# Attention: key, value and query-bias products on stacked rounded latents, and a one-pass transpose of the maxima

## The chip, the cores and the metric

One core of one Trainium2 chip runs the whole kernel in one launch. The metric is the device time of that launch in microseconds. Before the change three runs gave 646.17, 646.83 and 647.59 us; the median is 646.83 us. Engines are named as in the profile: PE (TensorE matmul), PEld (its weight loads), DVE (VectorE), ACT (ScalarE), POOL (GpSimd) and SP (which issues the DMAs).

## The reference

Two layers on x of 8 batches x 256 tokens x 128 features; each is an attention-like part and a feed-forward part of experts, under adaLN modulation. The change touches only the attention of layer 0:

```python
h = _layernorm(x, axis=-1) * (1 + ca) + sa
q = (h @ Wq + bq).reshape(B, T, H, D)                 # 16 heads of 8
kv_latent = gelu(h @ Wkd + bkd)                       # 64 wide
lat = kv_latent[..., :L] + kv_latent[..., L:]         # 32 wide
kv = lat @ Wku + bku
k, v = kv[..., :C].reshape(B, T, H, D), kv[..., C:].reshape(B, T, H, D)
attn = softmax(where(causal, q k^T / sqrt(8), -inf))
x = x + ga * ((attn @ v) @ Wo + bo)
```

The feed-forward part of layer 0 routes each token to 2 of 8 experts, beside a shared one (128 to 512 to 128, tanh gelu). Layer 1 is a gated linear recurrence with an MLP, and a second set of experts.

## The kernel before, in words

Everything lives in on-chip memory; features or heads lie on the 128 partitions and tokens along the free axis, in 4 blocks of 512. Each engine runs one instruction list in program order, written out by hand; semaphores join the lists. There is no scheduler, so the order of the source is the order on each engine.

An fp32 product costs TensorE several passes. Where the kernel wants fp32 quality for less, it splits an operand into a rounded part (type fp32r, one pass) and the rest, and adds the products of the parts: a copy into an fp32r tile rounds, and a subtraction of it from the original leaves the rest. `HH`/`HL` are the two parts of the hidden values, `WH`/`WL` those of an expert's weights, `LH`/`LL` those of the layer 1 weights, which lie in `M`.

Start. SP loads V, X (4 blocks), the modulation weights, `KM` (the key and value weights twice, and their bias row: 65 x 640), `M`, and more. PE takes means and variances; DVE centres (L669), copies the modulation out of PSUM (L839 to L851), and normalises block by block (L676, then L680 for each of the two batches in a block, which counts `hn_done`). PE makes the latent of a block (L1285, PSUM bank t), ACT its gelu into `LAT` (L421). Row 64 of `LAT` is one, so that the bias row of `KM` counts. POOL meanwhile sets up masks and identities, flips signs in `KM` (L282, L283; `flipped`) and in the query weights in `M` (L286, L287), rounds the layer 1 weights into `LH` (L289) and, after the second normalised block or later, makes `LL` (L292). PE then projects the first unit, and makes all values (L1400, 16 products of 128 columns, banks 2 to 5), which DVE adds to a bias row (L860). `keep_clock` (L1292) is a row of products whose result nobody reads.

A unit is one batch and 4 of the 16 heads; there are 32. `project` (L1298, L1299, bank 6) makes queries and keys of unit n+3 in plain fp32. ACT evacuates them four times (L432, L434, L436, L437): a kept copy `QKT`, in which only one row group of four survives, and a rounded copy `QKR`; the queries' bias comes in here from `KEPT` and `SIGNED`. POOL subtracts the two (L343, `join`) and so leaves stacked rows of rounded parts and rests, over which PE's `scores` (L1319, L1320) contract in one pass, in two halves h of two heads each in banks 0 and 1. DVE's `maxima` (L874) takes the row maxima of each half, and only then may PE write the next half. `spread_max` (L885, L887) puts the maxima, as rounded part and rest, into `MP`; PE turns them (L1373, `maxima_t`, an fp32 transpose against `IDF`); DVE adds them to the queries (L894, `with_max`). PE makes the transposed scores (L1333, L1334, and the mask L1337), ACT their exponentials (L444), PE the values' sums (L1349, L1352). DVE spreads the sums and divides (L900, L908), ACT takes the reciprocals (L456, L458). After the last units PE runs the output projection (L1364) and the second norm.

Experts of layer 0. POOL splits two experts' weights (L297, L300) and rounds the hidden blocks (L308); DVE takes the hidden rests (L692, `rest`), works out the routing (L768 and on), and takes the rests of the activations (L1015, `lower0`), for which PE waits before each second product.

## Time and profile before

| quantity | value |
|---|---|
| median of 3 runs | 646.83 us (646.17 to 647.59) |
| the profiled execution, whole | 646.88 us |
| its span, first to last instruction | 645.0 us |
| mean granted TensorE clock | 0.967 of full speed |
| busy PE, DVE, ACT, POOL | 599.1, 542.1, 487.6, 167.7 us |

The profiled execution took 646.88 us, of which 645.0 us is the span; the other 1.9 us lie around it. Busy times are sums over stages with different limits. The attention's units run from about 37 to 184 us, the first experts from about 204 us on. A row of the timeline says when an instruction starts, how long it takes, its engine, line and operation, and in brackets how long the engine had stood idle and on whom it waited.

### The profile page before, as it was taken

How to read it: one execution, taken by the hardware profiler on the slowest of the kernel's cores; microseconds unless marked ns; L12 is line 12 of the kernel's file. 1: busy time of each engine (PE TensorE's matmuls, PEld its weight loads, DVE VectorE, ACT ScalarE, POOL GpSimd, SP SyncE). 2: the span in 40 equal slices, each digit the busy share in tenths (PEclk: the TensorE clock that was granted, in tenths of full speed). 3: DMA queues.
4: the chain of work that ended last, by engine and by line, in shares of the span. 5: the costliest groups of instructions: out<-in, count | busy, mean ns of one | idle time of the engine just before them, and what ended most of it. 6: DMA issues, size and time to landing. Idle time of an engine off the chain costs nothing.

```text
span 645.0 us, 10999 instructions
## 1 busy us (share of the span) xinstructions
PE 599.1 (93%) x3297; PEld 441.4 (68%) x3297; DVE 542.1 (84%) x1338; ACT 487.6 (76%) x858; POOL 167.7 (26%) x144
## 2 busy tenths in 40 slices
PE   8799889888999999999999999785898999999996
PEld 5466556555545688888888888354675888888884
DVE  4868888888858868988988888869799789999997
ACT  5658999999647899999999999798635556666663
POOL 4422323223304033553455342040432000000000
PEclk9899999999998999999999999996897999999998
DMA  7000000000100042112201210000000222222201
GB/s 252 1 1 3 1 3 1 1 0 1 34 1 0 6 164 99 52 47 99 98 29 68 98 49 1 1 1 1 0 1 2 69 91 89 91 90 90 91 0 67
DMA packets 6491, 28.83 MB, mean 45 GB/s; under 512 B 862, under 2 KB 990, under 8 KB 4383
## 3 DMA queue, kind: packets, MB, share of 16 engines
q1 hardware_dynamic: 6448, 28.32, 12.4%
q8 instruction: 19, 0.31, 0.2%
q14 instruction: 24, 0.20, 0.1%
HBM read 27.13 MB, written 1.19 MB: 44 GB/s over the span
## 4 chain that ended last, share of the span: by engine, by line
PE 63%; DVE 24%; ACT 6%; issue 4%; DMA 1%; POOL 0%; SPq 0%; DVEq 0%; ACTq 0%; POOLq 0%
PE PS L1213 17%; PE PS L1215 16%; PE PS L1214 16%; DVE STAT L874 9%; PE PS L1364 2%; PE PS L1292 2%; DVE RA L894 2%; PE PS L1319 2%; PE PS L1239 2%; DVE SU L900 1%; DVE HN L680 1%; PE PS L1333 1%; ACT STAT L397 1%; DVE HL L692 1%; ACT RA L635 1%
## 5 line engine op out<-in xcount | busy, mean ns | idle before, releaser
L1015 DVE TENSOR_TENSOR RA<-AR,RA 128x512 fp32r<-128x512 f32 x144 | 137.4, 978 | 26.2 <-ACT RA L518 24.6
L517 ACT ACTIVATE AR<-PS,BI 128x512 f32<-128x512 f32 x144 | 99.8, 693 | 15.3 <-PE PS L1215 7.8
L1213 PE MATMUL PS<-HH,WH 128*128 128x512 f32 x272 | 108.9, 400 | 0.2
L1215 PE MATMUL PS<-HL,WH 128*128 128x512 f32 x272 | 107.1, 394 | 0.0
L1214 PE MATMUL PS<-HH,WL 128*128 128x512 f32 x272 | 107.1, 394 | 0.0
L518 ACT ACTIVATE RA<-PS,BI 128x512 fp32r<-128x512 f32 x144 | 98.7, 685 | 0.0
L874 DVE CUSTOM_DVE_ANT_0 STAT<-PS,MQ 128x128 f32<-128x128 f32 (+1 forms) x256 | 76.3, 355 | 20.0 <-PE PS L1320 19.9
L1213 PE MATMUL PS<-RA,WH 128*128 128x512 f32 x208 | 83.0, 399 | 3.7 <-DVE RA L1179 2.1
L1215 PE MATMUL PS<-RA,WH 128*128 128x512 f32 x208 | 81.2, 391 | 0.0
L1214 PE MATMUL PS<-RA,WL 128*128 128x512 f32 x208 | 81.2, 391 | 0.0
L320 POOL TENSOR_TENSOR AR<-AR 128x512 f32<-128x512 f32 x32 | 50.8, 1587 | 113.2 <-DVE AR L827 113.2
L343 POOL TENSOR_TENSOR RA<-QKT,RA 128x512 fp32r<-128x512 f32 x32 | 40.7, 1273 | 102.8 <-ACT RA L437 99.7
L635 ACT ACTIVATE RA<-AR 128x512 fp32r<-128x512 f32 x64 | 40.5, 633 | 32.8 <-DVE AR L1173 32.1
L1213 PEld LDWEIGHTS PS<-HH,WH 128*128 128x128 f32 x272 | 51.9, 191 | 12.8 <-issue 1.7
L1214 PEld LDWEIGHTS PS<-HH,WL 128*128 128x128 f32 x272 | 51.9, 191 | 11.1 <-issue 0.5
L1215 PEld LDWEIGHTS PS<-HL,WH 128*128 128x128 f32 x272 | 51.8, 190 | 11.1
L444 ACT ACTIVATE AR<-PS 128x768 f32<-128x768 f32 x64 | 48.5, 810 | 13.3 <-PE PS L1337 11.3
L629 ACT ACTIVATE AR<-PS 128x512 f32<-128x512 f32 x64 | 38.3, 598 | 20.7 <-PE PS L1215 19.2
L1213 PEld LDWEIGHTS PS<-RA,WH 128*128 128x128 f32 x208 | 39.1, 188 | 15.8 <-DVE RA L1015 5.1
L1179 DVE TENSOR_TENSOR RA<-AR,RA 128x512 fp32r<-128x512 f32 x64 | 44.2, 690 | 5.7 <-ACT RA L635 1.3
L1161 DVE TENSOR_TENSOR AR<-PS,AR 128x512 f32<-128x512 f32 x64 | 43.9, 687 | 4.2 <-ACT AR L629 3.6
L1215 PEld LDWEIGHTS PS<-RA,WH 128*128 128x128 f32 x208 | 39.2, 188 | 8.3
(212 smaller groups left out, 1164.3 us busy)
## 6 DMA issues: line engine op xcount, KB each, us to landing
...
```

Of the source, the lines that this page charges most:

```text
L320: gp.tensor_tensor(out=blk(ACC, t), in0=blk(ACC, t), in1=YW[:, t % 2, :], op=ALU.add)\
L444: act.activation(PR[:, n0 % 2, 2 * h:2 * h + 2, :], PS[:, 2 + 2 * h:4 + 2 * h, 0:384], ACT.Exp, scale=SCALE).then_inc(exp_done, 1)
L517: act.activation(G[:, c, :], PS[:, c, :], ACT.Gelu_apprx_tanh, bias=bias).then_inc(s["act"], 1)
L518: act.activation(GH[:, m0 % 2, c, :], PS[:, c, :], ACT.Gelu_apprx_tanh, bias=bias)\
L635: act.activation(GH[:, m % 2, c, :], G[:, c, :], ACT.Copy).then_inc(s1["gh"], 1)
L874: mm = dve.tensor_tensor_reduce(out=MASKED_S[:, q, j, 0:width], in0=PS[:, j, first:first + width], in1=MQ[:, 256 - width:256], scale=-1.0, ...
L1015: dve.tensor_tensor(out=GL[:, m0 % 2, c, :], in0=G[:, c, :], in1=f(GH[:, m0 % 2, c, :]), op=ALU.subtract).then_inc(s["lo"], 1)
L1161: dve.tensor_tensor(out=G[:, c, :], in0=PS[:, 2 + c, :], in1=SG[:, c, :], op=ALU.mult)\
L1179: dve.tensor_tensor(out=GL[:, m % 2, c, :], in0=G[:, c, :], in1=f(GH[:, m % 2, c, :]), op=ALU.subtract).then_inc(s1["lo"], 1)
L1213: pe.matmul(out, wh, xh, start=first, stop=False)
L1214: pe.matmul(out, wl, xh, start=False, stop=False)
L1215: return pe.matmul(out, wh, xl, start=False, stop=last)
```

## The change

The rounded parts and rests of the latents are made once, instead of multiplying keys and values in plain fp32 for each unit.

- `kmats` grows from 65 x 640 to 98 x 1250: three stacked copies of the key and value weights and two bias rows, the queries' bias in rows 96 and 97 of columns 640 to 1151, and a 0/1 matrix `pick` in the last 98 columns. `KM` now lies in the big tile AR.
- POOL flips signs in the queries' bias too, and splits that bias (three operations of 512 columns and two small ones). DVE splits the key and value weights into `KMS` (two operations of 640 columns), ahead of the copy of the modulation.
- The gelu's output goes to `LG`. A new product, `three_rows`, multiplies it by `pick` in plain fp32 and so adds the two halves of the latent and stacks them three times (98 rows, over the latent's bank). DVE's new `latents` reads that twice and leaves rounded parts and rests in `LAT`.
- `project` is the query's fp32 product, plus a one-pass product of the bias rows into the same bank, plus a one-pass key product. The values' 16 products are one-pass.
- ACT evacuates a unit in three operations instead of four: no bias, and both rounded copies in one operation of 512 columns.
- `maxima_t` multiplies `MP` by a rounded identity `IDR` in one pass.
- `LL` is no longer made at the start but on POOL after the last hidden block of the first experts has been rounded.

The diff, without the packing of the inputs on the host and the declarations:

```diff
@@ gpsimd
+            gp.wait_ge(ident_done, 9)
+            gp.tensor_scalar(IDR, IDF[:, :], 1.0, 0.0, ALU.mult, ALU.add).then_inc(ident_done, 1)
...
+            qb = KM[:, 640:1152].rearrange("p (h r c) -> p h r c", r=4, c=8)
+            gp.tensor_scalar(qb[:, :, 0, :], qb[:, :, 0, :], -1.0, 0.0, ALU.mult, ALU.add).then_inc(qk_bias, 1)
+            gp.tensor_scalar(qb[:, :, 2:4, :], qb[:, :, 2:4, :], -1.0, 0.0, ALU.mult, ALU.add).then_inc(qk_bias, 1)
+            gp.wait_ge(in_vec, 16)
+            gp.wait_ge(qk_bias, 2)
+            gp.tensor_scalar(KMR[:, 640:1152], KM[:, 640:1152], vec("w_sign")[0:98, :], 0.0, ALU.mult, ALU.add).then_inc(qk_bias, 1)
+            gp.tensor_scalar(KM[:, 640:1152], KM[:, 640:1152], vec("w_keep")[0:98, :], 0.0, ALU.mult, ALU.add).then_inc(qk_bias, 1)
+            gp.wait_ge(qk_bias, 4)
+            gp.tensor_tensor(out=KMS[:, 640:1152], in0=KM[:, 640:1152], in1=f(KMR[:, 640:1152]), op=ALU.subtract)\
+              .then_inc(qk_bias, 1)
...
-            gp.wait_ge(l1_split, 1)
-            gp.wait_ge(hn_done, 8)
-            gp.tensor_tensor(out=LL[:, :], in0=lm, in1=f(LH[:, :]), op=ALU.subtract).then_inc(l1_split, 1)
...
             split_weights(0, 1, 1, 1024)
             split_hidden(1, HN, 3)
+            gp.wait_ge(l1_split, 1)
+            gp.tensor_tensor(out=LL[:, :], in0=lm, in1=f(LH[:, :]), op=ALU.subtract).then_inc(l1_split, 1)
             experts(0, E0, 1024)
@@ scalar, evac_proj
-                act.activation(QKT[:, 0, :], PS[:, 6, 0:256], ACT.Identity,
-                               bias=KEPT[:, g:g + 1], scale=vec("q_keep")).then_inc(qk_evac, 1)
-                act.activation(QKR[:, 0, :], PS[:, 6, 0:256], ACT.Identity,
-                               bias=SIGNED[:, g:g + 1]).then_inc(qk_evac, 1)
+                act.activation(QKT[:, 0, :], PS[:, 6, 0:256], ACT.Copy, scale=vec("q_keep")).then_inc(qk_evac, 1)
                 act.activation(QKT[:, 1, :], PS[:, 6, 256:512], ACT.Copy, scale=vec("k_keep")).then_inc(qk_evac, 1)
-                act.activation(QKR[:, 1, :], PS[:, 6, 256:512], ACT.Copy).then_inc(qk_evac, 1)
+                act.activation(QKR[:, :, :], PS[:, 6, :].rearrange("p (k n) -> p k n", k=2), ACT.Copy).then_inc(qk_evac, 2)
@@ vector
             for t in range(NBLK):
                 centre(0, t)
+            dve.wait_ge(flipped, 2)
+            dve.tensor_scalar(KMR[:, 0:640], KM[:, 0:640], vec("w_sign")[0:98, :], None, ALU.mult).then_inc(kms_done, 1)
+            dve.wait_ge(kms_done, 1)
+            dve.scalar_tensor_tensor(out=KMS[:, 0:640], in0=KM[:, 0:640], scalar=vec("w_keep")[0:98, :], in1=f(KMR[:, 0:640]),
+                                     op0=ALU.mult, op1=ALU.subtract).then_inc(kms_done, 1)
...
+            def latents(t):
+                dve.wait_ge(sel_psum, t + 1)
+                if t >= 1:
+                    dve.wait_ge(l_done, t)
+                dve.tensor_scalar(LATR, PS[0:98, t, :], vec("lat_sign")[0:98, :], None, ALU.mult).then_inc(lr_done, 1)
+                dve.wait_ge(lr_done, t + 1)
+                dve.scalar_tensor_tensor(out=blk(LAT, t), in0=PS[0:98, t, :], scalar=vec("lat_keep")[0:98, :],
+                                         in1=f(LATR), op0=ALU.mult, op1=ALU.subtract).then_inc(l_done, 1)
+            for t in range(NBLK):
+                latents(t)
@@ tensor
+            def three_rows(t):
...
+                pe.wait_ge(lat_done, t + 1)
+                pe.matmul(PS[0:98, t, :], KM[0:65, 1152:1250], blk(LG, t), start=True, stop=True).then_inc(sel_psum, 1)
+            for t in range(3):
+                latent(t)
+            three_rows(0)
+            latent(3)
+            three_rows(1)
+            three_rows(2)
@@ project
-                pe.matmul(PS[:, 6, 0:256], mat("wq", g), HN[:, cols], start=True, stop=True)
-                pe.matmul(PS[:, 6, 256:512], KM[:, 128 * g:128 * g + 128], LAT[:, cols], start=True, stop=True)\
+                pe.matmul(PS[:, 6, 0:256], mat("wq", g), HN[:, cols], start=True, stop=False)
+                pe.matmul(PS[:, 6, 0:256], KMS[:, 640 + 128 * g:768 + 128 * g], LAT[:, cols], start=False, stop=True)
+                pe.matmul(PS[:, 6, 256:512], KMS[:, 128 * g:128 * g + 128], LAT[:, cols], start=True, stop=True)\
@@ maxima_t
-                    mm = pe.transpose(PS[:, 7, 256 + 128 * q:384 + 128 * q], f(MP[:, q, :]), IDF[:, :])
+                    mm = pe.matmul(PS[:, 7, 256 + 128 * q:384 + 128 * q], MP[:, q, :], IDR, start=True, stop=True)
@@ before the first unit
-            pe.wait_ge(lat_done, 1)
+            pe.wait_ge(kms_done, 2)
+            pe.wait_ge(qk_bias, 5)
+            pe.wait_ge(l_done, 1)
             project(0, 0, 0)
-            pe.wait_ge(lat_done, 4)
+            three_rows(3)
             for i in range(16):
+                if i % 4 == 0:
+                    pe.wait_ge(l_done, min(i // 4 + 3, 4))
```

POOL before, from the arrival of `KM` to the first join; AR and RA are the big tiles in which the new `KM`, `KMS` and `KMR` lie.

```order
L282 TENSOR_SCALAR KM<-KM 65x16x16 [waits in_k]
L283 TENSOR_SCALAR KM<-KM 65x16x8
L286 TENSOR_SCALAR M<-M 128x16x8 [waits in_mats]
L287 TENSOR_SCALAR M<-M 128x16x16
L289 TENSOR_SCALAR LH<-M 128x1664
L292 TENSOR_TENSOR LL<-M,LH 128x1664 [waits hn_done,l1_split]
L343 TENSOR_TENSOR RA<-QKT,RA 128x512 [waits qk_evac] x4
```

POOL after, the same place.

```order
L290 TENSOR_SCALAR AR<-AR 98x16x16 [waits in_k]
L291 TENSOR_SCALAR AR<-AR 98x16x8
L293 TENSOR_SCALAR AR<-AR 98x16x8
L294 TENSOR_SCALAR AR<-AR 98x16x16
L297 TENSOR_SCALAR RA<-AR,V 98x512 [waits qk_bias,in_vec]
L298 TENSOR_SCALAR AR<-AR,V 98x512
L300 TENSOR_TENSOR RA<-AR,RA 98x512 [waits qk_bias]
L304 TENSOR_SCALAR M<-M 128x16x8 [waits in_mats]
L305 TENSOR_SCALAR M<-M 128x16x16
L307 TENSOR_SCALAR LH<-M 128x1664
L358 TENSOR_TENSOR RA<-QKT,RA 128x512 [waits qk_evac] x4
```

Five operations on `KM` and the queries' bias now stand ahead of the query weights and `LH`, and `LL` is gone from here.

DVE before, from the last centring to the first normalised block.

```order
L669 TENSOR_TENSOR XC<-X,PS 128x512 [waits mean_done] x3
L839 COPY MOD<-PS 128x96 [waits mod_psum]
L840 TENSOR_SCALAR MC<-PS 128x32
L843 TENSOR_SCALAR GS<-MOD 128x32 [waits mod_done]
L845 SCALAR_TENSOR_TENSOR GA<-MOD 128x16 x2
L849 TENSOR_SCALAR GA<-GA 128x32 [waits gate_done]
L851 SCALAR_TENSOR_TENSOR MG<-GS,GA 128x32 [waits gate_done]
L676 TENSOR_TENSOR HN<-XC,STAT 128x512 [waits rstd_done]
L680 TENSOR_SCALAR HN<-HN,MC,MOD 128x256 [waits nrm_done]
```

DVE after, the same place.

```order
L681 TENSOR_TENSOR XC<-X,PS 128x512 [waits mean_done] x3
L848 TENSOR_SCALAR RA<-AR,V 98x640 [waits flipped]
L850 SCALAR_TENSOR_TENSOR RA<-AR,V,RA 98x640 [waits kms_done]
L855 COPY MOD<-PS 128x96 [waits mod_psum]
L856 TENSOR_SCALAR MC<-PS 128x32
L859 TENSOR_SCALAR GS<-MOD 128x32 [waits mod_done]
L861 SCALAR_TENSOR_TENSOR GA<-MOD 128x16 x2
L865 TENSOR_SCALAR GA<-GA 128x32 [waits gate_done]
L867 SCALAR_TENSOR_TENSOR MG<-GS,GA 128x32 [waits gate_done]
L688 TENSOR_TENSOR HN<-XC,STAT 128x512 [waits rstd_done]
L692 TENSOR_SCALAR HN<-HN,MC,MOD 128x256 [waits nrm_done]
```

The two operations of 640 columns stand between the centring and the copy of the modulation, and wait for POOL's `flipped`.

POOL before, from the last unit's neighbours to the first experts.

```order
L300 TENSOR_TENSOR WL<-WS,WH 128x1024 [waits moe0_split]
L308 TENSOR_SCALAR HH<-HN 128x512 [waits hn_done] x3
L297 TENSOR_SCALAR WH<-WS 128x1024 [waits moe0_w_in]
L300 TENSOR_TENSOR WL<-WS,WH 128x1024 [waits moe0_split]
L308 TENSOR_SCALAR HH<-HN 128x512 [waits hn_done]
L320 TENSOR_TENSOR AR<-AR 128x512 [waits moe0_ymul,moe0_acc_init]
```

POOL after, the same place.

```order
L315 TENSOR_TENSOR WL<-WS,WH 128x1024 [waits moe0_split]
L323 TENSOR_SCALAR HH<-HN 128x512 [waits hn_done] x3
L312 TENSOR_SCALAR WH<-WS 128x1024 [waits moe0_w_in]
L315 TENSOR_TENSOR WL<-WS,WH 128x1024 [waits moe0_split]
L323 TENSOR_SCALAR HH<-HN 128x512 [waits hn_done]
L374 TENSOR_TENSOR LL<-M,LH 128x1664 [waits l1_split]
L335 TENSOR_TENSOR AR<-AR 128x512 [waits moe0_ymul,moe0_acc_init]
```

`LL`, a subtraction of 1664 columns with both inputs in SBUF, stands right behind the rounding of the last hidden block, which DVE's `rest` of that block waits for.

## Rows read from the trace of the kernel before

**Rows 1.** Waits, 57 to 166 us: who waited for whom, us, times, longest.

```profile
DVE STAT L874 <- PE PS L1320: 15.0, 25, 0.6
PE PS L1319 <- DVE NM L874: 4.7, 25, 0.2
```

**Rows 2.** Timeline, one unit; start, us, engine, line; idle in brackets.

```profile
102.20 0.29 DVE L874 CUSTOM_DVE_ANT_0 STAT<-PS,MQ 128x128 f32<-128x128 f32 x1 [0.60 <-PE PS L1320]
...
103.43 0.18 DVE L885 CAST MP<-NM 128x8 fp32r<-128x8 f32 x1
...
103.49 0.60 PE L1299 MATMUL PS<-AR,KM 65*128 x2
...
103.93 0.39 PE L1373 MATMUL PS<-IDF,MP 128*128 128x128 f32 x2
...
104.44 0.41 DVE L894 TENSOR_TENSOR RA<-RA,PS 128x256 fp32r<-128x256 f32 x1
...
107.82 0.17 DVE L885 CAST MP<-NM 128x8 fp32r<-128x8 f32 x1
```

**Rows 3.** Timeline, end of the units, POOL and DVE.

```profile
170.45 2.35 POOL L300 TENSOR_TENSOR WL<-WS,WH 128x1024 fp32r<-128x1024 f32 x1
170.50 2.32 DVE L887 TENSOR_TENSOR MP<-NM,MP 128x8 f32<-128x8 f32 x1
```

**Rows 4.** Timeline, the start, POOL and DVE.

```profile
11.85 0.40 POOL L282 TENSOR_SCALAR KM<-KM 65x256 f32<-65x256 f32 x1 [6.08 <-DMA KM<-in_kmats]
...
13.82 0.26 DVE L839 COPY MOD<-PS 128x96 f32<-128x96 f32 x1 [3.78 <-PE PS L1276]
...
14.97 0.79 POOL L286 TENSOR_SCALAR M<-M 128x128 f32<-128x128 f32 x1 [2.46 <-DMA M<-in_mats]
15.64 2.21 DVE L680 TENSOR_SCALAR HN<-HN,MC,MOD 128x256 f32<-128x256 f32 x2
...
16.10 1.61 POOL L289 TENSOR_SCALAR LH<-M 128x1664 fp32r<-128x1664 f32 x1
...
21.23 0.73 DVE L680 TENSOR_SCALAR HN<-HN,MC,MOD 128x256 f32<-128x256 f32 x2
...
22.12 3.70 POOL L292 TENSOR_TENSOR LL<-M,LH 128x1664 fp32r<-128x1664 f32 x1 [4.41 <-DVE HN L680]
22.14 3.70 DVE L949 SCALAR_TENSOR_TENSOR SP<-V,SP 128x1 f32<-128x1 f32 x1
```

**Rows 5.** Chain that ended last, 28 to 36 us: start, us, what.

```profile
28.58 0.33 PE PS L1319 x2
...
30.17 0.57 ACT QKT L432
...
31.80 1.18 PE PS L1298 x2
...
33.83 2.56 PE PS L1292 x8
```

**Rows 6.** Busy time by stretch: us; PE, PEld, DVE, ACT, POOL; PEclk, DMA, GB/s.

```profile
11.00:15.00 4.00, 4.00 (x28) 3.30 (x28) 1.07 (x8) 3.03 (x6) 0.69 (x3) 0.98 0.83 332
28.00:32.00 4.00, 2.32 (x14) 1.51 (x14) 2.89 (x16) 1.57 (x4) 0.55 (x2) 0.98 0.00 0
32.00:35.00 3.00, 3.00 (x8) 2.36 (x9) 1.32 (x4) 1.13 (x3) 1.15 (x1) 0.50 0.00 0
```

**Rows 7.** Timeline, the first experts' start.

```profile
208.34 0.62 POOL L308 TENSOR_SCALAR HH<-HN 128x512 fp32r<-128x512 f32 x1 [2.01 <-DVE HN L680]
...
208.99 0.69 DVE L692 TENSOR_TENSOR HL<-HN,HH 128x512 fp32r<-128x512 f32 x1 [0.74 <-POOL HH L308]
...
210.13 0.68 DVE L1015 TENSOR_TENSOR RA<-AR,RA 128x512 fp32r<-128x512 f32 x1
...
210.87 0.50 PE L1213 MATMUL PS<-RA,WH 128*128 128x512 f32 x1 [0.69 <-DVE RA L1015]
```

**Rows 8.** Busy time by stretch, as rows 6.

```profile
212.00:216.00 4.00, 3.78 (x17) 2.52 (x16) 3.81 (x13) 4.00 (x9) 0.00 (x0) 1.00 0.00 0
```

More of the change, by code:

```diff
@@ L12 @@
 MASKED = -1e30
[L15 to L16 removed]
+VECS = dict(bo=1, q_keep=1, k_keep=1, b1=4 * E0, b2=E0, pb=4, gb=3, fb=3,
+            outb=1, alpha=1, norm=1, norm2=1, bkd=1, c=16, prio=8,
+            w_sign=1, w_keep=1, lat_sign=1, lat_keep=1)
 MATS = dict(wkd=64, wq=512, wo=512, router=8, wg=8, l1=4 * 128 + 3 * 384)
@@ L92, in build @@
         ON = AR[:, 0:8192].rearrange("p (g n) -> p g n", g=4)
-        LAT = AR[0:65, 8192:10240]
+        LG = AR[0:65, 8192:10240]
+        KM = AR[0:98, 2048:3298]
         VALL = AR[:, 10240:12288].rearrange("p (i c) -> p i c", i=16)
@@ L102, in build @@
         QKR = RA[:, 2560:3072].rearrange("p (k n) -> p k n", k=2)
+        IDR = RA[:, 7936:8064]
+        LAT = RA[0:98, 3072:5120]
+        KMS = RA[0:98, 5120:6272]
+        KMR = RA[0:98, 6272:7424]
+        LATR = RA[0:98, 7424:7936]
         MASKED_S = STAT[:, 0:1024].rearrange("p (q j n) -> p q j n", q=2, j=2)
         QKT = sb("QKT", [128, 2, 256])
-        KEPT = sb("KEPT", [128, 4])
-        SIGNED = sb("SIGNED", [128, 4])
         NM = sb("NM", [128, 8])
@@ L420, in _ @@
                 act.wait_ge(kd_done, t + 1)
-                act.activation(LAT[0:64, t * BLK:(t + 1) * BLK], PS[0:64, t, :], ACT.Gelu, bias=vec("bkd")[0:64, :])\
+                act.activation(LG[0:64, t * BLK:(t + 1) * BLK], PS[0:64, t, :], ACT.Gelu, bias=vec("bkd")[0:64, :])\
                    .then_inc(lat_done, 1)
             def evac_proj(n, g):
-                if isinstance(n, int) and n == 0:
-                    act.wait_ge(qk_bias, 2)
                 act.wait_ge(proj_done, n + 1)
@@ L886, in spread_max @@
                 dve.wait_ge(mp_ready, 2 * n + 1)
-                dve.tensor_tensor(out=f(MP[:, :, 25::32]), in0=nmv, in1=f(MP[:, :, 24::32]),
+                dve.tensor_tensor(out=MP[:, :, 25::32], in0=nmv, in1=f(MP[:, :, 24::32]),
                                   op=ALU.subtract).then_inc(mp_ready, 1)
@@ L1282, in _, with latent @@
             pe.wait_ge(in_mats, 16)
-            for t in range(NBLK):
+            def latent(t):
                 pe.wait_ge(hn_done, 2 * t + 2)
@@ L1286, in _ @@
                   .then_inc(kd_done, 1)
+            def three_rows(t):
+                if t == 0:
+                    pe.wait_ge(in_k, 16)
+                    pe.wait_ge(latent_one, 1)
+                pe.wait_ge(lat_done, t + 1)
[6 more added lines that the diff above has]
+            three_rows(2)
             def keep_clock(count, bank=7):
@@ L1681, in layouts @@
     put("bkd", a["L0_attn_bkd"])
+    put("w_sign", np.repeat(np.array([-1, -1, 1, -1, 1], f4), [32, 32, 32, 1, 1]))
+    put("w_keep", np.repeat(np.array([0, 0, 1, 0, 1], f4), [32, 32, 32, 1, 1]))
+    put("lat_sign", np.repeat(np.array([-1, 1, -1, -1], f4), [32, 32, 32, 2]))
+    put("lat_keep", np.repeat(np.array([0, 1, 0, 0], f4), [32, 32, 32, 2]))
     put("c", np.concatenate([a["L0_c"], a["L1_c"]]).T)
@@ L1694, in layouts @@
     wk = np.concatenate([heads(a["L0_attn_Wku"][:, :128], 3).reshape(32, 512), a["L0_attn_Wku"][:, 128:]], 1)
+    bias = np.concatenate([bk.reshape(1, 512), np.zeros((1, 128), f4)], 1)
+    pick = np.zeros((98, 98), f4)
+    pick[np.arange(192) % 64, np.arange(192) // 64 * 32 + np.arange(192) % 32] = 1.0
+    pick[64, 96:98] = 1.0
+    qb = np.concatenate([np.zeros((96, 512), f4), np.tile(heads(a["L0_attn_bq"], 3).reshape(1, 512), (2, 1))])
     rows = np.concatenate([a["L0_attn_bku"][128:], a["L0_ffn_router_b"]])
```

19 lines of the change are left out of this document (5 added, 14 removed).

## The prediction, made before the changed kernel was run

> **What bounds the kernel now.** I read four views, in this order. The waits over the middle of the attention say who stands still: DVE's `maxima` waits for the second half of the scores once a unit, 25 times in 109 us, 0.60 us each [rows 1, 2]; no other wait of DVE is among the long ones. The timeline of one unit says why: from one L885 to the next it takes 4.39 us (103.43 to 107.82), and DVE is busy in all of it but those 0.60 us. The wait is a round trip: PE may write the second half only when the first half's maxima are taken, and PE itself stands idle before that product (4.7 us in 25 times, 0.2 each) [rows 1]. So DVE plus this round trip is the period, not PE, though PE is the busiest engine of the page. Third, the start of the program, where the order of POOL and DVE decides. Fourth, the start of the first experts, where DVE is busy 3.81 of 4 us, ACT 4.00 and PE 3.78 [rows 8]: nobody has room there.
>
> **The loop.** Per unit PE loses a key product in plain fp32 (0.43 us from L1299 to L1373 [rows 2]) and gains two one-pass products of 256 columns. Eight such products of 512 columns took at least 2.56 us, half of it at half clock [rows 5, 6], so one of 256 costs at most 0.16; PE saves 0.11 to 0.43, I take 0.2. ACT saves an instruction of four, 0 to 0.41 (a quarter of the 1.63 us from 30.17 to 31.80 [rows 5]), I take 0.15. The one-pass transposes end at most some 0.3 us earlier. DVE's instructions are the same ones. The turned maxima are wanted at 104.44, when DVE comes to L894 without a wait; PE started on them at 103.93 [rows 2]. Being earlier there is worth nothing, and being later by more than a few tenths would cost; a 128-column product on the same operands doesn't look slower. The 0.60 us round trip consists of scores alone, which don't change. So the loop is worth 0 (between -0.1 and +0.1 us a unit, 3 us either way over 28 units), and the saved PE and ACT time becomes idle time.
>
> **Two engines, one path to SBUF.** The costs below rest on a behaviour that the trace shows three times. At the end of the units DVE's subtraction of 8 columns, 0.17 us elsewhere, took 2.32 us, exactly as long as POOL's `WL` beside it [rows 3]. L949 on one column took 3.70 us beside POOL's `LL` of 3.70 [rows 4]. And two L680, 0.73 us later on, took 2.21 beside POOL's `LH` [rows 4]. The small instruction waited for all of the large one. The Trainium skill says so too (SBUF — State Buffer, "SBUF: two separate sides"): an exclusive lock, held for the whole instruction by whoever starts first, against a DVE instruction with two SBUF inputs or in a two-port mode. The trace agrees; were it a sharing of bandwidth, `LL` would stretch its neighbours by tenths, not by microseconds.
>
> **The start, step by step.** (1) `KM` grows from 162.5 to 478.5 KB and `M` lies behind it in SP's queue. At 332 GB/s [rows 6] that is 1.0 us: `KM` at 12.8 instead of 11.85, `M` at 15.9 instead of 14.97 [rows 4]. (2) POOL now has, between the two, four small sign flips (0.40 for 256 columns [rows 4]; 1.2 in all), two operations of 512 columns (1.61 x 512/1664 = 0.5 each) and a subtraction (3.70 x 512/1664 = 1.1): 3.3 us; then as before the query flips and `LH`, 2.2 us. (3) DVE gets two operations of 640 columns (0.69 x 640/512 = 0.86 each [rows 7]), which wait for `flipped`, some 13.4 at the earliest. Queued behind them are the copy of the modulation (13.82 before [rows 4]), five small operations on it, and the first normalised block, for which PE and everything later wait. Lower end: 13.4 + 1.7 = 15.1, 1.3 us later than 13.82. Upper end: every such DVE instruction takes turns with a POOL one, 12.8 + 5.5 + 1.7 + 1.4 (normalising) + 0.6 (small ones) = 22.0 against 17.85 before, 4.2 later. Walking both queues with turns I come to 21.1, so +3.2: the small operations each let one of POOL's by, and `LH` falls, as before, into the first block. (4) The last block is then normalised at 25.2 instead of 21.96. From there the first scores took 6.6 us (28.58 [rows 5]). Now a stacking product must come first (1.4 us until PE has got to it, behind a latent at half clock), then DVE's eight operations of 512 columns, 0.69 each and a semaphore between, 5.7 us, of which the value products wait for the last, and 12 of these, 1.2 us at 0.1: 8.3 us, at most, 7.4 where the stacking product is ready. I take 8.1: +1.5. No cover for it: ACT's evacuation and POOL's join of unit 0 are done by then. What goes is `LL` beside L949, which nobody waited for. (5) Up to the first unit, two projections and one evacuation are on the path: -0.2, -0.2, -0.2. The filler products behind them ran at half clock in part, after a stretch in which PE was busy 2.32 of 4 us [rows 6]; if the clock stays up, 1.3 us more go, if it falls longer, as much is lost. I take -0.6. The start: 3.2 + 1.5 - 0.6 = **+4.1**, from +1 to +6.
>
> **The end of the units.** POOL reaches the experts' first weights some 0.3 us earlier, so the 2.32 us of blocking [rows 3] begin and end earlier: **-0.3** (0 to -0.5).
>
> **`LL` at its new place.** It takes 3.70 us with its port [rows 4] and starts when L308 ends, at 208.96; DVE's L692 for the same block is released by the same event and started at 208.99 [rows 7]. If POOL is first, L692 ends 3.6 us later. If DVE is first, L692, a product read out of PSUM and a reduction pass, and L1015 at 210.13, with both inputs in SBUF, waits till 213.1: 3.0. Behind L1015 stand the routing and all further L1015; PE waited for this very one, 0.69 us until 210.87 [rows 7]. DVE, ACT and PE are full from there on [rows 8], so nothing catches up: I take **+3.3**. PE then stands idle nearly 4 us. When it had been busy 2.32 us of 4 the granted clock went to 0.50, the 1.2 GHz level, for about 3 us [rows 6]; the same here costs up to half of 3.4 us of PE's work, and PE sets the pace: **+1.0** (0 to +2.5). The Trainium skill (TensorE: Matmul & The Clock Gate, "HAM oscillation — how this bites in real kernels") speaks of the same: an engine that has to wait restarts cold, and the wait is paid again. The trace agrees, with these rows.
>
> **The sum** against the profiled execution: 646.88 (645.0 of span and 1.9 around it, at the median of the runs, 646.83) + 4.1 + 0 - 0.3 + 3.3 + 1.0 = 655.0 us.
>
> **Rivals.**
>
> *A, the block at the experts is hidden.* `LL` meets no DVE instruction that needs the path, or the engines have more room than rows 8 say. Only the start remains: 646.9 + 4.1 - 0.3 + 0.3 = 651.0. For it: PE idled 0.69 us there. Against it: three blocked instructions in rows 3 and 4.
>
> *B, the start is cheap.* The small operations pass POOL, data arrive no later, and the new DVE work fills the 3.78 us in which DVE stood idle before 13.82 [rows 4]: +1 in place of 4.1, 651.9. Against it: that idle time is mostly over when `KM` arrives.
>
> *C, the loop is bound by PE after all.* Every unit DVE is released by PE [rows 1]; if what ends the 0.60 us is PE's queue and not the round trip, the wait shrinks by what PE saves, up to 0.4 us with both edits. Over 28 units that is -11.2: 646.9 + 8.1 - 11.2 = 643.8, faster than before. It decides from 0.3 us a unit. Against it are PE's own 0.2 us of idleness just before [rows 1].
>
> *D, the clock falls again.* With less PE work per unit, a long wait for the last latent and the idle stretch at the experts, two or three more stretches at half clock: +4, 659. For it: it fell after 2.32 of 4 us. Against it: in the units PE is still busy most of the time.
>
> **How the numbers follow.** The forecast 0.56, A 0.13, B 0.14, C 0.07, D 0.10. The forecast's own range is 653 to 657.5. Eight in ten, with A and B taken in and part of D: 649.8 to 659. A difference of 0.2% (1.3 us) is about what these measurements tell from none. Faster: C, 0.07. The same: the gentle end of B with A, 0.04. Slower: 0.89.
>
> **What would show it.** In the changed profile: the copy of the modulation at 15 us or later, POOL and DVE in turns with instructions stretched up to the neighbour's end, and the first normalised block 1.3 to 4.2 us late; the first scores at 33 us (28.58 before); a unit still of 4.39 us with the 0.60 us wait in it, and new idle time of PE before the transposes and of ACT before its evacuation; `LL` at the experts' start beside an L692 or L1015 (under their new line numbers) of over 3.5 us, a PE that waits for it some 4 us, and a clock at 0.50 behind it. A unit shorter than 4.2 us would prove me wrong in the loop, and first scores before 31 us in the start.

## The result, and the profile after

The changed kernel takes 658.29 us, median of 4 runs (657.57 to 659.06), against 646.69 us for the kernel before in the same session (646.17 to 647.59): ratio 1.0178, 95% interval 1.0160 to 1.0196. It is slower, by 11.6 us. The forecast was 655.0, 8.1 us slower; its own range was 653 to 657.5, the wider one, with parts of the rivals in it, 649.8 to 659. Some single executions of the changed kernel's variants have a long stretch at a lower clock; the ratios leave them out, and of `a4_rows`, whose profiled execution was such a one from 123 us on, only the start is read.

The profiled execution took 658.58 us, span 656.7, mean clock 0.960. When the same event comes in both traces (line before / line after):

| event | before | after | difference |
|---|---|---|---|
| POOL's first flip, `KM` has landed (L282 / L290) | 11.85 | 13.51 | +1.7 |
| first block normalised (end of the second L680 / L692) | 17.85 | 21.84 | +4.0 |
| last block normalised | 21.96 | 25.95 | +4.0 |
| first maxima (L874 / L904) | 29.11 | 37.09 | +8.0 |
| last unit's maxima leave (L885 / L915) | 178.21 | 185.89 | +7.7 |
| first activation rest (L1015 / L1042) | 210.13 | 221.29 | +11.2 |
| the 61st of these | 292.35 | 305.04 | +12.7 |
| end of the span | 645.0 | 656.7 | +11.7 |

So 8.0 us arise ahead of the first maxima, 0.3 come back over the units, 3.5 arise at the experts' start, 1.5 just behind it, and 1.0 comes back later.

These are differences of two single traces, and the start scatters. In the eight profiled kernels whose start is the old one or nearly so (the kernel before and, of the experiments below, `b1_ll_late`, `b2_load`, `b3_turn`, `c1_early`, `c2_placed`, `e1_nokey` and `e2_dve`) the first maxima come at 28.9 to 31.3 us, and the trace of the kernel before, with 29.11, is one of the early ones; after the change they come at 37.1. From the first maxima to the end of the span it takes 619.4 to 619.7 us in the three kernels that make `LL` at the experts (the changed one, `a3_both_late`, `b1_ll_late`) and 614.7 to 616.8 in the eight that make it at the start and whose loop and experts are not slowed or rearranged otherwise (`before`, `a1_ll_back`, `a5_all`, `b2_load`, `b3_turn`, `b5_split`, `c1_early`, `e1_nokey`). The two places of loss stand clear of this scatter; single microseconds in the table don't.

The start, timeline, POOL and DVE; it answers to [rows 4]: start, length, engine, line, and in brackets the idle time and its releaser.

```profile
13.51 0.41 POOL L290 TENSOR_SCALAR AR<-AR 98x256 f32<-98x256 f32 x1 [7.34 <-DMA AR<-in_kmats]
...
14.21 0.57 DVE L848 TENSOR_SCALAR RA<-AR,V 98x640 fp32r<-98x640 f32 x1 [2.34 <-POOL AR L291]
14.82 0.89 DVE L850 SCALAR_TENSOR_TENSOR RA<-AR,V,RA 98x640 fp32r<-98x640 f32 x1
15.63 0.24 DVE L855 COPY MOD<-PS 128x96 f32<-128x96 f32 x1
...
17.03 1.31 POOL L300 TENSOR_TENSOR RA<-AR,RA 98x512 fp32r<-98x512 f32 x1
17.13 3.94 DVE L688 TENSOR_TENSOR HN<-XC,STAT 128x512 f32<-128x512 f32 x1
...
18.95 1.58 POOL L307 TENSOR_SCALAR LH<-M 128x1664 fp32r<-128x1664 f32 x1
```

DVE's first normalising operation, 0.69 us elsewhere, takes 3.94. It starts 0.10 us after POOL's L300 and ends 0.54 us after POOL's L307 has ended (20.53). Between them POOL ran four instructions in a row (L300, L304, L305, L307), and DVE got in between none of them. The prediction had reckoned with turns.

From the last block to the first maxima, timeline, PE and DVE.

```profile
27.00 1.10 PE L1322 MATMUL PS<-AR 65*98 65x512 f32 x2
...
28.14 0.75 DVE L879 TENSOR_SCALAR RA<-PS,V 98x512 fp32r<-98x512 f32 x1 [2.19 <-PE PS L1322]
...
34.25 0.75 DVE L881 SCALAR_TENSOR_TENSOR RA<-PS,V,RA 98x512 fp32r<-98x512 f32 x1
...
35.06 1.55 PE L1446 MATMUL PS<-RA 98*128 98x128 f32 x12 [0.99 <-DVE RA L881]
...
36.54 0.33 PE L1363 MATMUL PS<-RA 32*128 32x128 f32 x2
...
37.09 0.29 DVE L904 CUSTOM_DVE_ANT_0 STAT<-PS,MQ 128x128 f32<-128x128 f32 x1 [0.59 <-PE PS L1364]
```

DVE waits 2.19 us for the first stacking product, then does the eight operations of `latents` from 28.14 to 35.00, and the last twelve value products and the scores stand behind them. The clock shows in the busy times by stretch (us; PE, PEld, DVE, ACT, POOL; clock, DMA share, GB/s), the second row of which answers to the ladder at half clock in [rows 6]:

```profile
22.00:26.00 4.00, 4.00 (x5) 1.07 (x6) 3.84 (x9) 1.01 (x2) 0.00 (x0) 0.50 0.00 0
...
36.00:44.00 8.00, 7.31 (x29) 5.71 (x29) 4.47 (x20) 2.65 (x6) 2.08 (x2) 0.57 0.01 3
217.00:222.00 5.00, 0.82 (x4) 0.35 (x3) 4.97 (x6) 2.08 (x4) 3.29 (x1) 0.58 0.00 0
222.00:226.00 4.00, 3.97 (x9) 3.17 (x10) 3.76 (x13) 2.28 (x4) 0.00 (x0) 0.50 0.00 0
```

The loop, waits from 65 to 174 us, who waited for whom (total, times, longest); it answers to [rows 1]:

```profile
DVE STAT L904 <- PE PS L1364: 15.0, 25, 0.6
ACT AR L456 <- PE PS L1381: 14.2, 25, 0.6
...
PE PS L1363 <- DVE NM L904: 4.6, 25, 0.2
```

and one unit of it, timeline, as [rows 2]:

```profile
102.33 0.17 DVE L915 CAST MP<-NM 128x8 fp32r<-128x8 f32 x1
...
102.85 0.43 PE L1417 MATMUL PS<-RA,MP 128*128 128x128 f32 x2
...
103.60 0.41 DVE L924 TENSOR_TENSOR RA<-RA,PS 128x256 fp32r<-128x256 f32 x1
...
106.95 0.18 DVE L915 CAST MP<-NM 128x8 fp32r<-128x8 f32 x1
...
111.33 0.17 DVE L915 CAST MP<-NM 128x8 fp32r<-128x8 f32 x1
```

DVE waits for the scores the same 15.0 us in 25 units, a unit takes 4.38 us (106.95 to 111.33; the one before it, 4.62, has the placing of new values in it), and what ACT has saved has become a wait of its own, 14.2 us. The turned maxima are ready at 103.28, and L924 comes at 103.60, when DVE gets to it.

The end of the units, timeline, as [rows 3]:

```profile
177.80 2.35 POOL L315 TENSOR_TENSOR WL<-WS,WH 128x1024 fp32r<-128x1024 f32 x1
178.03 2.15 DVE L915 CAST MP<-NM 128x8 fp32r<-128x8 f32 x1
```

The small operation waits for the split as before, another line and 0.17 us less.

The first experts, timeline, as [rows 7]:

```profile
216.59 3.71 POOL L374 TENSOR_TENSOR LL<-M,LH 128x1664 fp32r<-128x1664 f32 x1
216.66 4.18 DVE L704 TENSOR_TENSOR HL<-HN,HH 128x512 fp32r<-128x512 f32 x1 [0.74 <-POOL HH L323]
...
221.29 0.68 DVE L1042 TENSOR_TENSOR RA<-AR,RA 128x512 fp32r<-128x512 f32 x1
...
222.03 0.80 PE L1240 MATMUL PS<-RA,WH 128*128 128x512 f32 x1 [4.20 <-DVE RA L1042]
```

POOL was first; the rest of the last hidden block (0.69 us before) took 4.18, and PE stood 4.20 us for the operation behind it (0.69 before).

### The profile page after: what moved, and what is told of

The parts are those of the page before. It is cut to its first block, busy times and chain, and to the rows that moved or that the text cites. A ratio compares the mean times of both kernels' runs of the same rounds, so it can differ in the third digit from the quotient of the medians.

```text
span 656.7 us, 10968 instructions
## 1 busy us (share of the span) xinstructions
PE 601.9 (92%) x3289; PEld 445.7 (68%) x3289; DVE 551.2 (84%) x1346; ACT 478.7 (73%) x826; POOL 171.0 (26%) x150
## 4 chain that ended last, share of the span: by engine, by line
PE 63%; DVE 24%; ACT 6%; issue 5%; DMA 2%; SPq 0%; POOL 0%; DVEq 0%; ACTq 0%
PE PS L1240 17%; PE PS L1241 16%; PE PS L1242 16%; DVE STAT L904 9%; PE PS L1408 2%; PE PS L1335 2%; DVE RA L924 2%; PE PS L1363 2%; DMA AR<-in_kmats 2%; DVE HN L688 1%; DVE SU L930 1%; DVE HL L704 1%; ACT STAT L414 1%; PE PS L1377 1%; PE PS L1266 1%
## 5 line engine op out<-in xcount | busy, mean ns | idle before, releaser
L1042 DVE TENSOR_TENSOR RA<-AR,RA 128x512 fp32r<-128x512 f32 x144 | 137.7, 980 | 25.9 <-ACT RA L530 24.5
L904 DVE CUSTOM_DVE_ANT_0 STAT<-PS,MQ 128x128 f32<-128x128 f32 (+1 forms) x256 | 76.2, 354 | 19.1 <-PE PS L1364 19.1
L456 ACT ACTIVATE AR<-PS 128x768 f32<-128x768 f32 x64 | 48.4, 809 | 24.1 <-PE PS L1381 24.1
L1240 PEld LDWEIGHTS PS<-HH,WH 128*128 128x128 f32 x272 | 51.9, 191 | 12.7 <-issue 1.9
L1241 PEld LDWEIGHTS PS<-HH,WL 128*128 128x128 f32 x272 | 52.0, 191 | 10.6 <-issue 0.2
```

The lines of the kernel that those rows point to most:

```text
L456: act.activation(PR[:, n0 % 2, 2 * h:2 * h + 2, :], PS[:, 2 + 2 * h:4 + 2 * h, 0:384], ACT.Exp, scale=SCALE).then_inc(exp_done, 1)
L904: mm = dve.tensor_tensor_reduce(out=MASKED_S[:, q, j, 0:width], in0=PS[:, j, first:first + width], in1=MQ[:, 256 - width:256], scale=-1.0, ...
L1042: dve.tensor_tensor(out=GL[:, m0 % 2, c, :], in0=G[:, c, :], in1=f(GH[:, m0 % 2, c, :]), op=ALU.subtract).then_inc(s["lo"], 1)
L1240: pe.matmul(out, wh, xh, start=first, stop=False)
L1241: pe.matmul(out, wl, xh, start=False, stop=False)
```

## The experiments

Each ratio is against the kernel before, timed beside it on the same chip. `a` is an edit of the changed kernel, `b`, `c` and `e` of the kernel before.

### b1_ll_late, the move of `LL` alone

```diff
-            gp.wait_ge(l1_split, 1)
-            gp.wait_ge(hn_done, 8)
-            gp.tensor_tensor(out=LL[:, :], in0=lm, in1=f(LH[:, :]), op=ALU.subtract).then_inc(l1_split, 1)
...
             split_hidden(1, HN, 3)
+            gp.wait_ge(l1_split, 1)
+            gp.tensor_tensor(out=LL[:, :], in0=lm, in1=f(LH[:, :]), op=ALU.subtract).then_inc(l1_split, 1)
```

> The kernel before with nothing changed but the place of LL, behind the last hidden block of the first experts. Theory (exclusive path): +3.5 us for the blocked subtraction, and 0 to +1.6 for the clock: 650.2 to 652, with an L692 of over 4 us beside it. Rival 1 (it only hurts in the changed kernel, whose phases differ): 646.5 to 647.5. Rival 2 (bandwidth is shared, the neighbours stretch by tenths): 647 to 647.7.

Measured: 651.12 us, ratio 1.0053 (1.0030 to 1.0077), 3.4 us slower. Its timeline:

```profile
211.09 3.71 POOL L356 TENSOR_TENSOR LL<-M,LH 128x1664 fp32r<-128x1664 f32 x1
211.16 4.19 DVE L691 TENSOR_TENSOR HL<-HN,HH 128x512 fp32r<-128x512 f32 x1 [0.74 <-POOL HH L305]
...
215.80 0.68 DVE L1014 TENSOR_TENSOR RA<-AR,RA 128x512 fp32r<-128x512 f32 x1
```

The operation behind starts 4.64 us after the rest does, against 1.14 before [rows 7], and the price is passed on nearly whole. For the clock behind it little is left: from the first to the 61st activation rest it takes 82.8 us, against 82.2 before (up to 82.6 in other kernels with `LL` at the start) and 83.8 after the change.

### a1_ll_back, everything but the move of `LL`

The same edit backwards, on the changed kernel.

> The changed kernel with LL made on POOL at the start again, behind LH and the second normalised block. Theory (the exclusive path between POOL and DVE, and the clock behind it): the 4.18 us L704 falls to about 0.7, the 4.20 us in which PE waited at the first experts go, and so does the half clock behind it: 3.5 us for the wait and 1.6 for the clock, 653.2 us (652.5 to 654.5). At the start LL now lies beside DVE's latents, which read PSUM and one tile of SBUF: nothing is blocked there. Rival 1 (the engines catch up elsewhere, LL is a symptom): 657.5 to 658.5. Rival 2 (LL blocks the latents just as it blocked the rest): what is won at the experts is lost at the start, 657 to 658, and an L879 or L881 of 3 to 4 us.

Measured: ratio 1.0127 (1.0082 to 1.0172), so some 3.3 us of the 11.6 are gone, with a wide interval; the theory had 5. The timeline at the experts:

```profile
218.47 0.69 DVE L705 TENSOR_TENSOR HL<-HN,HH 128x512 fp32r<-128x512 f32 x1 [0.74 <-POOL HH L326]
...
219.61 0.68 DVE L1043 TENSOR_TENSOR RA<-AR,RA 128x512 fp32r<-128x512 f32 x1
```

The block is away, and from the first maxima (38.12) to here it takes 181.5 us, as before (181.0); after the change it is 184.2. `LL` waits for the fourth normalised block (`hn_done` counts two for each), so at the start it now ran from 27.31 to 31.01, beside the first operations of `latents`, and these kept their 0.75 us. They have one operand in PSUM. The Trainium skill (SBUF — State Buffer, "SBUF: two separate sides") says that a DVE operation with two inputs in SBUF, or in a two-port mode, and a POOL operation shut each other out. The trace agrees for the inputs: 0.75 here, 4.18 where both were in SBUF.

### a3_both_late, the splitting moved behind the normalising

```diff
-            dve.wait_ge(flipped, 2)
-            dve.tensor_scalar(KMR[:, 0:640], ...)
-            dve.scalar_tensor_tensor(out=KMS[:, 0:640], ...)
             dve.wait_ge(mod_psum, 1)
...
             for t in range(NBLK):
                 normalise(0, t)
+            (the same lines)
```

and POOL's five operations on the queries' bias behind `LH`.

> The changed kernel with two moves at the start: DVE's two operations on the key weights stand behind the fourth normalised block, where DVE waited 2.19 us for the first stacking product, and POOL's split of the queries' bias (two flips, two operations of 512 columns, one subtraction) stands behind LH. Theory (the run of POOL instructions held the path and DVE's L688 waited 3.94 us for all of it): L688 is then at most some 2 us long, the first normalised block is ready 2.5 to 3.5 us earlier, and the whole is 655 us (654.3 to 656). Rival 1 (the start is bound by the arrival of the inputs): at most 0.5 us is won, 657.8 to 658.3. Rival 2 (the latents' chain on DVE and the half clock bind): the earlier first block is given back behind it, 656.8 to 658.

Measured: 658.21 us, ratio 1.0164 (1.0136 to 1.0192): no gain that can be told from none, though the first block was normalised 4.1 us earlier (17.72). The timeline says where it went:

```profile
18.36 2.22 DVE L692 TENSOR_SCALAR HN<-HN,MC,MOD 128x256 f32<-128x256 f32 x2
...
23.08 2.02 DVE L692 TENSOR_SCALAR HN<-HN,MC,MOD 128x256 f32<-128x256 f32 x2
...
25.59 0.88 DVE L871 SCALAR_TENSOR_TENSOR RA<-AR,V,RA 98x640 fp32r<-98x640 f32 x1
26.39 0.74 DVE L879 TENSOR_SCALAR RA<-PS,V 98x512 fp32r<-98x512 f32 x1
...
32.91 2.82 PE L1446 MATMUL PS<-RA 98*128 98x128 f32 x12 [0.98 <-DVE RA L881]
...
36.51 0.29 DVE L904 CUSTOM_DVE_ANT_0 STAT<-PS,MQ 128x128 f32<-128x128 f32 x1 [1.75 <-PE PS L1364]
```

Most of it is lost before the last block: two pairs of normalising operations, 0.73 us elsewhere, now wait beside `LH` (18.82 to 20.43) and beside POOL's moved splitting (to 24.94), and the last block is ready at 25.09, only 0.9 us earlier. The two DVE operations then stand between it and `latents`, which end at 32.85, and the value products behind ran at half clock, 2.82 us instead of 1.55. The first maxima are 0.6 us earlier. This is the second rival's outcome, by a longer road.

### b5_split, the splitting alone, on the kernel before

```diff
+            gp.wait_ge(flipped, 2)
+            gp.tensor_scalar(<128 columns>) ; gp.tensor_scalar(<256 columns>)
+            gp.tensor_scalar(<512 columns>) ; gp.tensor_scalar(<512 columns>)
+            gp.tensor_tensor(<512 columns>, op=ALU.subtract)
...
+            dve.wait_ge(flipped, 2)
+            dve.tensor_scalar(RA[0:65, 6272:6912], KM[:, 0:640], 1.0, None, ALU.mult).then_inc(kms_done, 1)
+            dve.wait_ge(kms_done, 1)
+            dve.scalar_tensor_tensor(out=RA[0:65, 5120:5760], in0=KM[:, 0:640], scalar=1.0,
+                                     in1=f(RA[0:65, 6272:6912]), op0=ALU.mult, op1=ALU.subtract).then_inc(kms_done, 1)
             dve.wait_ge(mod_psum, 1)
```

> The kernel before, with the new splitting work alone: behind POOL's sign flips two small copies, two copies of 512 columns and a subtraction of 512, and on DVE, ahead of the copy of the modulation, a rounding and a subtraction of 640 columns that wait for the flips. Their results go to unused columns and are read by nobody. Nothing is loaded in addition, so KM lands as before. Theory 1 (the queue at the start is the mis-sized part, and it is passed on whole): the first normalise of the first block takes over 3 us beside POOL's row of instructions, the first normalised block is 3 to 4.5 us late, the last one as well, and the time is 3 to 4.5 us longer, 650 to 651.5 us. Theory 2 (the start is dear only through the chain over the latents): the first block is late by 1 to 4 us but the time is at most 1.5 us longer.

Measured: 649.17 us (12 runs), ratio 1.0019 (1.0004 to 1.0033): 1.2 us. Theory 1 has fallen, theory 2 holds. Its timeline:

```profile
11.49 0.40 POOL L283 TENSOR_SCALAR KM<-KM 65x256 f32<-65x256 f32 x1 [5.71 <-DMA KM<-in_kmats]
...
12.91 0.89 DVE L851 SCALAR_TENSOR_TENSOR RA<-KM,RA 65x640 fp32r<-65x640 f32 x1
16.06 0.26 DVE L855 COPY MOD<-PS 128x96 f32<-128x96 f32 x1 [2.25 <-PE PS L1292]
...
16.45 2.00 DVE L859 TENSOR_SCALAR GS<-MOD 128x32 f32<-128x32 f32 x1
```

`KM` lands at 11.49, as in the kernel before, and both DVE operations are over before the modulation is there; DVE even waits 2.25 us for it. What is left is one small operation that waited for POOL, 2.00 us for 32 columns. The first block is normalised at 20.41, 2.6 us later than in the trace of the kernel before, but 1.2 later than in the middle one of the eight with the old start (17.6 to 20.0, median 19.2), which is what the times say. After the change, with `KM` at 13.51, it is 21.84.

### b2_load and a4_rows, the load

`b2_load` is the kernel before with `KM` padded to 128 x 896, 448 KB. `a4_rows` is the changed kernel with `kmats` padded from 98 to 128 rows of the same 5000 bytes, 625 KB.

> The kernel before with a larger load for KM (128 x 896 elements, 448 KB instead of 162.5; the added columns and rows are zeros and are not used). Theory (the load takes its share of the channel from those issued ahead of it and behind it): the last block of X, KM and M arrive about 1 us later; M alone gates nothing for long, the modulation product is up to 1.5 us later and with it the first normalised block: +0.5 to +1.5 us, 647.3 to 648.3. Rival (loads behind each other in the queue are served in order and DVE waits for something else anyway): 646.5 to 647.0. If it is over 649, the load is the main cost of the start.

> The changed kernel with the KM load padded from 98 to 128 rows of 5000 bytes (625 KB instead of 478.5), on the 128 partitions that the other loads have; the added rows are zeros. The 448 KB load of 128 rows cost the kernel before nothing and landed at 11.3 us, while the 98-row load landed at 13.4 to 14.4. Theory (the 98-row shape, not its bytes, makes the start late, because the first blocks of X and the modulation weights also arrive 1 to 2 us late with it): KM lands at 12 to 12.5, the last centring ends before 10.5 instead of 11.9, the whole 656.5 to 657.5. Rival (bytes): 0.5 us later than the changed kernel, 658.5 to 659.5. Rival (the start's lateness is on DVE and POOL alone): 658 to 658.5.

Measured: `b2_load` 647.3 us, ratio 0.9998 (0.9971 to 1.0026), the weights there at 11.32. `a4_rows` 1.0155 (1.0118 to 1.0191); the weights were there at 11.64, and the first maxima at 35.67, 1.4 us earlier than after the change. The last centring did not end earlier as forecast, but at 12.45. The busy time by stretch from 9 to 12.75 us, columns as above, shows the loads; after the change:

```profile
9.00:12.75 3.75, 3.75 (x11) 1.63 (x9) 2.06 (x3) 1.32 (x2) 0.00 (x0) 1.00 1.02 248
```

and in `a4_rows`:

```profile
9.00:12.75 3.75, 3.75 (x8) 1.62 (x7) 2.36 (x4) 0.81 (x3) 1.10 (x4) 1.00 1.03 434
```

While the load of 98 rows was under way, all loads together moved 248 GB/s, with 128 rows 434, though these carry more bytes. Four profiled executions with 98 rows had the weights at 13.51, 14.44, 14.72 and 15.38; none with 65 or 128 rows had them later than 12.62. So at 5000 bytes a row it is the 98 rows that make them late, not the size. The Trainium skill (DMA: Bandwidth & Descriptors, "Why a DMA increments its semaphore by 16 and not by 1") says that a transfer is dealt to the largest number of engines up to 16 that divides its outer dimension: 14 for 98 rows, 16 for 128. The trace doesn't bear that out as the whole cause: the DMA share of 1.02, against 1.03, shows no idle engines; 14 of 16 of 434 would still be 380; and 65 rows, 13 engines by the same rule, weren't late. Why 98 rows are slow stays open. How much of the 11.6 us it is stays open too: the total differs from the changed kernel's by less than the intervals tell.

### a5_all, the three moves undone together

> The changed kernel with all three moves undone together: LL at the start behind LH, DVE's splitting of the key and value weights behind the normalising, POOL's splitting of the bias behind LH. What is left of the change is the stacking, the latents, the one-pass products, the evacuation in three instructions and the larger load. If the excess of 11.6 us is the sum of its parts (LL and the clock behind it 5, the queue ahead of the first block 1 to 4): 650 to 653 us, still 3 to 6 us slower than before, because the latents' chain stays and the loop gives nothing. Rival (the loop's savings are only covered up by the three moves): 647 us or less. Second rival (the moves trade places with one another and the queue merely reappears): 656 us or more.

Measured: 657.7 us, ratio 1.0169 (1.0130 to 1.0208), the second rival. Timeline, POOL and DVE:

```profile
26.18 3.87 POOL L310 TENSOR_TENSOR LL<-M,LH 128x1664 fp32r<-128x1664 f32 x1 [0.29 <-DVE HN L693]
26.54 4.20 DVE L872 SCALAR_TENSOR_TENSOR RA<-AR,V,RA 98x640 fp32r<-98x640 f32 x1
...
40.88 0.29 DVE L905 CUSTOM_DVE_ANT_0 STAT<-PS,MQ 128x128 f32<-128x128 f32 x1 [1.75 <-PE PS L1365]
```

and its busy time by stretch, columns as above:

```profile
32.00:49.00 17.00, 15.34 (x48) 11.51 (x48) 10.22 (x30) 3.98 (x9) 3.82 (x3) 0.50 0.01 1
```

`LL` left the experts and met the moved subtraction of the key weights, both of whose inputs are in SBUF: 4.20 us, right ahead of `latents`. PE stood idle for 3.28 us meanwhile, until 32.33, and its clock was at half from 31.9 us for 17 us. From the first maxima on this variant is as fast as the kernel before (181.5 us to the first activation rest, 184.2 after the change); up to them it is 11.8 us later.

### e1_nokey, b3_turn and e2_dve, who sets the loop

`e1_nokey` leaves out the key product from the fifth unit on; `b3_turn` takes the one-pass transposes alone; `e2_dve` adds a copy to DVE in 28 units:

```diff
+                if n0 >= 4:
+                    dve.tensor_copy(STAT[:, 1024:1152], MQ[:, 0:128])
```

> The kernel before; from the fifth unit on the key product is left out (queries and keys of the later units are then not those of the reference), so PE has 0.43 us less to do in each of 28 units, more than the change saves it, and the same is queued on all other engines. Theory (a unit is DVE's work plus a round trip of 0.60 us): the period stays 4.39 us, the whole 646.2 to 647.5. Rival (PE's queue sets the unit): up to 0.4 us less in each of 28 units, 635 to 640.

> The kernel before, with the one-pass transposes of the maxima alone (one rounded identity more on POOL early in the start, and DVE leaves the maxima's rest in a rounded type). Forecast: DVE is the engine that sets the unit, and comes to the turned maxima without a wait, so the period stays 4.38 to 4.40 us and the time within 0.2% of before, 646 to 648 us. Rival (what DVE waits for in its 0.6 us is PE's queue): the transposes are 0.1 to 0.3 us shorter a unit, the time falls by 3 to 8 us.

> The kernel before with one more DVE copy of 128 columns in each of the last 28 units, behind L894; its result is not used. Theory (DVE sets the unit): its 0.15 to 0.22 us is paid in every unit, 4.39 becomes 4.55 to 4.6 us, the whole 651 to 653. Rival (the unit has room on DVE, PE or ACT sets it): 646.5 to 647.5.

Measured: `e1_nokey` 0.9996 (0.9980 to 1.0013), `b3_turn` 0.9997 (0.9980 to 1.0014), `e2_dve` 1.0042 (1.0025 to 1.0058), 2.7 us slower. One row of the timeline each a unit apart; `e1_nokey`:

```profile
103.22 0.17 DVE L885 CAST MP<-NM 128x8 fp32r<-128x8 f32 x1
107.60 0.17 DVE L885 CAST MP<-NM 128x8 fp32r<-128x8 f32 x1
```

`b3_turn`:

```profile
100.26 0.17 DVE L889 CAST MP<-NM 128x8 fp32r<-128x8 f32 x1
104.65 0.18 DVE L889 CAST MP<-NM 128x8 fp32r<-128x8 f32 x1
```

`e2_dve`:

```profile
101.74 0.17 DVE L885 CAST MP<-NM 128x8 fp32r<-128x8 f32 x1
106.23 0.17 DVE L885 CAST MP<-NM 128x8 fp32r<-128x8 f32 x1
```

Less work for PE leaves the period at 4.38 and 4.39 us; one small operation more on DVE makes it 4.49. That is less than the forecast of 4.55 to 4.6: the copy takes 0.22 us, but the next operation starts 0.13 after it, and the 0.60 us wait stays. DVE with its round trip sets the loop, and rival C has fallen.

### c1_early and c2_placed, the second expert's split on the kernel before

```diff
             split_weights(0, 0, 0, 1024)
-            for t in range(3):
+            gp.wait_ge(moe[0]["w_in"], 32)
+            split_weights(0, 1, 1, 1024)
+            for t in range(4):
                 split_hidden(1, HN, t)
-            gp.wait_ge(moe[0]["w_in"], 32)
-            split_weights(0, 1, 1, 1024)
-            split_hidden(1, HN, 3)
```

`c1_early` is this. `c2_placed` also makes the first expert's split behind the first join instead of behind the last, and the second's only when all maxima have left.

> The kernel before with POOL's two weight splits of the first experts moved: the first expert's from behind the last join to behind the first, where DVE works from PSUM; the second's from between the hidden blocks to behind the last unit's L887. Theory (exclusive path): L887 takes 0.17 instead of 2.32 us, the three L692 2.1 instead of 4.94 us, together 4 to 5 us, part of it in places where PE was the later one: 642.5 to 644. Rival 1 (PE's output projections bind there): 645.5 to 647. Rival 2 (the split behind join 0 delays the first units by as much): 645 to 646.5.

> The kernel before; POOL splits the second expert's weights right behind the first's, ahead of the first three hidden blocks, instead of behind them. The variant that did this and also moved the first expert's split into the attention took 645.6 us, 0.997 of before. If its gain is the freed way for the last hidden block at the experts' start: this one gains as well, 0.5 to 1.5 us. If the gain is the first expert's split no longer beside DVE's small instructions at the end of the units: this one gains nothing, or loses up to 2 us, since both splits now stand beside them.

Measured: `c2_placed` 645.62 us (10 runs), ratio 0.9968 (0.9953 to 0.9982): 2.1 us faster than the kernel before, so it beats both, though the theory had 3 to 4.5. `c1_early` 0.9998 (0.9980 to 1.0017): nothing. A row of the timeline of each; `c1_early`:

```profile
180.58 2.56 DVE L907 TENSOR_TENSOR AR<-OT,SU 128x256 f32<-128x256 f32 x1
```

`c2_placed`:

```profile
203.39 1.93 DVE L690 TENSOR_TENSOR HL<-HN,HH 128x512 fp32r<-128x512 f32 x3
```

In `c2_placed` the first expert's split runs at 31.05 us, where DVE has no operation with two SBUF inputs beside it, and the three hidden rests wait for nothing (1.93 us instead of 4.94). In `c1_early` they wait for nothing either, but the operation of [rows 3] still does (2.33 us), and the second expert's split, at 180.50 us, now meets another DVE operation with two SBUF inputs, the one shown: 2.56 us instead of 0.42.

What such a wait costs depends on who is late there. That of [rows 3] costs nothing: from the last cast of the maxima but one to the last it takes 7.9 us with it (`before`, `c1_early`) and without it (`c2_placed`). The 3.0 us at the hidden rests bring 0.5: from the last unit's maxima to the first activation rest it takes 31.4 us in `c2_placed` and 31.9 in the kernel before. The new wait costs 1.1: in `c1_early` it takes 32.5. The rest of the gain of `c2_placed` lies behind, where the clock from 430 to 470 us is 0.91 instead of 0.83; but it is 0.91 in `c1_early` as well, so this part isn't settled.

## Why the prediction was right, and where a size was off

The direction, the places of the losses and the wider range held; the sum was 3.6 us short, and the forecast's own range, up to 657.5, was missed. The step that failed in size is the start: it had +4.1, "from +1 to +6", and the first scores at 33 us; measured are +8.0 against the trace of the kernel before, with the first scores at 36.54 us. That the total still lies inside the wider range, by 0.7 us, is in part luck: its upper end had been put there for rival D, whose mechanism this wasn't. Term by term:

- **The loop, 0**: right. The 0.60 us wait and the period stayed, and the three experiments on it show that DVE and its round trip set it. The "idle time of ACT before its evacuation" came at its exponentials instead, L456.
- **`LL` at its new place, +3.3**: right, 3.5 in the trace, and 3.4 with all that follows where it was moved alone. It went the way of the first case, POOL first.
- **The clock behind it, +1.0**: 1.5 in the trace, inside its bounds, but at most 0.5 where `LL` was moved alone. The granted clock fell to 0.50, the 1.2 GHz level, at 217.8 us, when PE's wait began (before, from 214 to 217.8, PE had been busy 2.08 us of 3.8), and rose at 228.1, 6 us after PE had work again.
- **The end of the units, -0.3, and the ladder, -0.6**: together -0.3 (8.0 ahead of the first maxima, 7.7 at the last unit's). The ladder gave nothing: the clock was at half there from 36.9 to 43.7 us, where before it had been so from 31.9 to 35.3.
- **The start's first part, +3.2**: 4.0. Two readings of step (3) were wrong. `KM` landed at 13.51, not at 12.8, since bytes over rate is not what the load goes by. And POOL and DVE did not take turns: L688 waited through four instructions in a row. The small operations, for their part, hardly waited.
- **The start's second part, +1.5**: this is the term that was mis-sized most. It was 4.0 (8.0 less 4.0). Step (4) had 8.1 us from the last block to the first scores where there had been 6.6; it was 10.6. DVE waited 2.19 us for the stacking product and not 1.4, because PE made the latents ahead of it at half clock (0.50 from 22 to 26 us); the eight operations took 6.9 and not 5.7, at 0.75 each and with 0.50 of waiting for the second product; and the twelve value products took 1.55 and not 1.2.

What the experiments add is that these parts don't add up freely. Putting the splitting elsewhere gave the first block its 4.1 us back and the total nothing (`a3_both_late`), undoing all three moves made the start worse (`a5_all`), and the splitting alone costs 1.2 us where `KM` is early (`b5_split`). The chain over stacking product, `latents` and value products is in every variant of the change. From the last normalised block to the first maxima it takes 10.9 to 11.4 us in these (14.8 in `a5_all`, with the blocked subtraction in it), and 6.8 to 7.2 in all kernels without it, `b5_split` too. So this chain costs 4 us, about half of the 8.0, and that is the steadiest number of the start; a kernel with the stacking alone wasn't tried. Neither was one in which the values don't wait for it. The other half lies ahead of the last block, in the splitting and the late `KM`, and some of it is the early start of the trace that it is measured against.

Rival B, the start cheap, holds for the splitting if the weights are early (+1.2 in `b5_split`), but not for the whole. Rival D had the right total, 659, by another road: the three stretches at half clock in the start and at the experts were longer (10.2, 6.8 and 10.2 us instead of 6.8, 3.4 and 3.4), but the last of them cost 1.5 us, and the first two are a part of the start.
